# Graph attention layer on one core: all four parts of a strip as bf16 high halves on TensorE and low halves by DMA

## What is computed

```python
q = x @ Wq.T + bq; k = x @ Wk.T + bk; v = x @ Wv.T + bv
scores = q @ k.T / sqrt(128)
scores = where(adj > 0, scores, -9e15)
attention = softmax(scores, axis=-1)
return elu(attention @ v)

h = maximum(layernorm(x), 0)
x = x + L0(h, adj)
h = maximum(layernorm(x), 0)
x = x + L1(h, adj)
```

## Time and profile before

| | |
|---|---|
| median of 3 runs | 781.47 us (781.42 to 786.33) |
| profiled execution | 782.49 us, its span 780.7 us |
| busy in the span | TensorE 93%, VectorE 72%, ScalarE 72%, GpSimd 53% |
| mean granted TensorE clock | 0.977 |
| chain that ended last | third stage, matmuls of line 1337: 30% of the span |

### The profile page before, as it was taken

One profiled execution on the slowest core, in us unless ns is written; L12 is line 12 of the kernel. 1 busy time (PEld: TensorE's weight loads), 2 busy tenths in 40 slices (PEclk: granted clock), 3 DMA queues, 4 the chain that ended last, 5 costly groups with the idle time before them and its releaser, 6 DMA issues. The chain is left out here.

```text
span 780.7 us, 18250 instructions
## 1 busy us (share of the span) xinstructions
PE 728.9 (93%) x6229; PEld 609.6 (78%) x6229; DVE 563.2 (72%) x1199; ACT 559.9 (72%) x1095; POOL 417.6 (53%) x317
## 2 busy tenths in 40 slices
PE   4976999999999999999999998585999999999996
PEld 2555888888888888888888887463888888888885
DVE  4857687878787878878787876498585585586572
ACT  5936678687878777777868787584967977977910
POOL 1058599999999999999999973243000000000000
PEclk9988999999999999999999999797999999999999
DMA  6059989999888898989898954650234334423100
GB/s 229 1 162 280 283 212 248 274 232 280 233 280 238 271 253 254 262 247 256 255 259 245 274 112 73 123 103 1 54 69 93 81 73 91 91 64 87 37 10 13
DMA packets 189323, 130.86 MB, mean 168 GB/s; under 512 B 170336, under 2 KB 176992, under 8 KB 181088
## 3 DMA queue, kind: packets, MB, share of 16 engines
q1 hardware_dynamic: 188544, 130.05, 61.4%
q10 hardware_dynamic: 576, 0.26, 0.1%
q0 software_dynamic: 160, 0.00, 0.0%
HBM read 69.47 MB, written 18.87 MB: 113 GB/s over the span
## 5 line engine op out<-in xcount | busy, mean ns | idle before, releaser
L1337 PE MATMUL ps_x<-v,big 128*128 128x258 bf16 x2048 | 232.0, 275 | 2.3 <-issue 2.3
L1337 PEld LDWEIGHTS ps_x<-v,big 128*128 128x128 fp8e4 x2048 | 198.9, 98 | 32.5 <-issue 2.4
L682 DVE CUSTOM_DVE_ANT_0 scores<-ps_s,mask_neg 128x1024 f32<-128x1024 f32 x128 | 155.7, 1217 | 25.5 <-POOL mask_neg L553 17.0
L538 POOL TENSOR_SCALAR mask_bytes<-adj_sb 128x2048 uint8<-128x2048 int32 x64 | 147.5, 2321 | 44.8 <-POOLq L79 40.9
L601 ACT ACTIVATE scores<-scores,neg_max 128x1024 f32<-128x1024 f32 x128 | 146.1, 1143 | 23.3 <-DVE neg_max L688 23.3
L701 DVE TENSOR_TENSOR low<-scores 128x1024 bf16<-128x1024 f32 x96 | 136.0, 1417 | 29.2 <-ACT scores L601 27.0
L553 POOL TENSOR_SCALAR mask_neg<-mask_bytes 128x2048 bf16<-128x2048 uint8 x64 | 150.6, 2354 | 5.4 <-POOL mask_bytes L538 0.4
L812 PE MATMUL ps_acc<-v_parts,hiT 128*128 128x256 bf16 x768 | 141.6, 274 | 5.4 <-DMA lowT<-low 5.1
L615 ACT ACTIVATE hiT<-ps_t 128x512 bf16<-128x512 bf16 (+1 forms) x128 | 103.0, 805 | 56.6 <-PE ps_t L793 54.0
L878 ACT ACTIVATE big<-s_block,s_col 128x512 fp8e4<-128x512 f32 x224 | 139.3, 714 | 0.0
L813 PE MATMUL ps_acc<-v_parts,lowT 128*128 128x128 bf16 x768 | 134.7, 220 | 0.0
(11 more groups left out here) (139 smaller groups left out, 997.3 us busy)
## 6 DMA issues: line engine op xcount, KB each, us to landing
adj_sb<-in_adj SPq DMA_DIRECT2D x64, 1024.0 KB, 5.3
mask_bytes_dram<-mask_bytes SPq DMA_DIRECT2D x32, 512.0 KB, 2.8
x_sb<-in_x SPq DMA_DIRECT2D x8, 256.0 KB, 7.7
out<-res SPq DMA_DIRECT2D x32, 64.0 KB, 1.5
lowT<-low SPq DMA_TRANSPOSE x96, 4.7
big<-mask_bytes_dram SPq DMA_TRANSPOSE x32, 4.5
raw_w<-in_L_gnn_Wq ACTq DMA_DIRECT2D x1, 64.0 KB, 3.1
raw_w<-in_L_gnn_Wk ACTq DMA_DIRECT2D x1, 64.0 KB, 3.6
```

What stands on the lines that cost most here:

```text
L538: nc.gpsimd.tensor_scalar(mask_bytes[b % 2][:, half(h)], adj_sb[h][:], 1.0, 0.0, ALU.min, ALU.max).then_inc(bytes_ready, 1)
L682: nc.vector.tensor_tensor_reduce(out=scores[bn % 2][:, part(k)], in0=ps_s[k % 2][:], in1=mask[bn % 2][:, part(k)], scale=1.0, scalar=LOWES ...
L1337: last = nc.tensor.matmul(ps_x[b % 2][k][:], by_key_tile(m, t)[:, b], v1[k][:, t, :].bitcast(BF16), start=(t == 0), stop=(t == T - 1))
```

## The change

All four parts of a strip now go the way that parts 0 to 2 went: the bf16 high half is turned on TensorE (UNITS lists the six groups), the low half is made by `low_part` on VectorE and turned by DMA into `lowT`. `turn`, `copy_pT`, `turned_low` and their buffers are gone. `acc_copy` and `add_halves` are replaced by `attended` on VectorE: two operations that scale the two halves of `ps_acc` by the inverse sum out of PSUM and add v's bias. ELU's minus one is subtracted from x once, on GpSimd, while the stage starts, and the subtraction in `add_elu` goes.

```diff
+            UNITS = ((3, slice(0, 512)), (3, slice(512, PART)), (0, slice(0, PART)), (1, slice(0, PART)),
+                     (2, slice(0, 512)), (2, slice(512, PART)))
...
                     def turn_low(c, b, k):
 
                         s = 4 * c + b
-                        sp.wait_ge(low_done, 3 * s + k + 1)
+                        sp.wait_ge(low_done, 4 * s + 1 + (1, 2, 3, 0)[k])
...
-                            sp.wait_ge(pv_done, 8 * s + 2 * k - 4)
+                            sp.wait_ge(pv_done, 8 * s + (-4, -2, 0, -6)[k])
...
                         if has(c, b, 1):
+                            turn_low(*at(c, b, 1), 3)
                             turn_low(*at(c, b, 1), 0)
...
-                    def add_halves(s):
-
-                        pool.wait_ge(acc_out, s + 1)
...
-                        nc.gpsimd.tensor_tensor(acc_sb[:, 0, :], acc_sb[:, 0, :], acc_sb[:, 1, :], ALU.add).then_inc(halves_added, 1)
-                        pool.wait_ge(halves_added, s + 1)
-                        nc.gpsimd.tensor_tensor(att[:], acc_sb[:, 0, :], bv_rep[:], ALU.add).then_inc(att_ready, 1)
-
                     def add_elu(s):
 
-                        steps = Steps(pool, pool_own, 2 * s)
+                        steps = Steps(pool, pool_own, s)
                         pool.wait_ge(att_exp_ready, s + 1)
-                        steps.do(nc.gpsimd.tensor_tensor(att_exp[:], att_exp[:], ones[:], ALU.subtract))
                         steps.do(nc.gpsimd.tensor_tensor(att_exp[:], att_exp[:], att_pos[:], ALU.add))
...
                         make_bytes(0, b)
                         if b < 2:
                             make_mask(0, b)
+                        if b == 1:
+                            flat = x_sb[:].rearrange("p t f -> p (t f)")
+                            nc.gpsimd.tensor_scalar(flat, flat, 1.0, None, ALU.subtract)
...
-                        copy_pT(s, 0)
+                        copy_hiT(s, 0)
                         if has(c, b, 2):
                             copy_q(s + 2, b % 2)
-                        copy_pT(s, 1)
-                        if before:
-                            acc_copy(s - 1, b + 1)
-                        copy_hiT(s, 0)
                         copy_hiT(s, 1)
+                        copy_hiT(s, 2)
+                        copy_hiT(s, 3)
                         if ahead:
                             exps(s + 1, bn, 0)
-                        copy_hiT(s, 2)
+                        copy_hiT(s, 4)
...
-                        copy_hiT(s, 3)
+                        copy_hiT(s, 5)
...
+                    def attended(s):
+
+                        dve.wait_ge(pv_done, 8 * s + 8)
+                        nc.vector.scalar_tensor_tensor(out=acc_sb[:], in0=ps_a[:, 1, :], scalar=inv_by_parity[:, 0:1],
+                                                       in1=bv_rep[:], op0=ALU.mult, op1=ALU.add).then_inc(acc_half, 1)
+                        wait(dve, att_exp_ready, s)
+                        dve.wait_ge(acc_half, s + 1)
+                        nc.vector.scalar_tensor_tensor(out=att[:], in0=ps_a[:, 0, :], scalar=inv_by_parity[:, 0:1],
+                                                       in1=acc_sb[:], op0=ALU.mult, op1=ALU.add).then_inc(att_ready, 1)
...
-                        turned_low(s, 0)
                         low_part(s, b, 1)
                         if ahead:
                             add_mask(s + 1, bn, 2)
-                        turned_low(s, 1)
+                        if has(c, b, -1):
+                            attended(s - 1)
                         low_part(s, b, 2)
...
                         if ahead:
-                            low_part(s + 1, bn, 0)
+                            low_part(s + 1, bn, 3)
                         if ahead2:
                             add_mask(s + 2, (b + 2) % 4, 1)
+                        if ahead:
+                            low_part(s + 1, bn, 0)
...
                     def times_v(s, i):
                         j = PV_ORDER[i]
-                        if i < 2:
-                            pe.wait_ge(pT_low_ready, 2 * s + i + 1)
-                        else:
-                            pe.wait_ge(hiT_ready, 4 * s + (1, 1, 2, 2, 3, 4)[i - 2])
-                            if i % 2 == 0:
-                                pe.wait_ge(lowT_in[j // 2], 16 * s + 16)
+                        pe.wait_ge(hiT_ready, TURNS * s + (1, 2, 3, 3, 4, 4, 5, 6)[i])
+                        if i % 2 == 0:
+                            pe.wait_ge(lowT_in[j // 2], 16 * s + 16)
                         if i == 0:
-                            wait(pe, acc_out, s)
+                            wait(pe, att_ready, s)
...
-                        turn(s, b, 0)
+                        turn_high(s, b, 0)
...
-                        turn(s, b, 1)
+                        turn_high(s, b, 1)
...
-                        turn_high(s, b, 0)
+                        turn_high(s, b, 2)
                         times_v(s, 0)
-                        turn_high(s, b, 1)
+                        turn_high(s, b, 3)
                         times_v(s, 1)
```

More of the change, by code:

```diff
@@ L436, in build @@
                 scores = [sb(c2, f"scores{i}", [D, N], F32) for i in range(2)]
[L437 to L441, removed]
+                hiT = [sb(c2, f"hiT{k}", [D, PART], BF16) for k in range(4)]
+                low = [sb(c2, f"low{k}", [D, PART], BF16) for k in range(4)]
+                lowT = [sb(c2, f"lowT{k}", [D, 8, D], BF16) for k in range(4)]
                 q_strip = [sb(c2, f"q_strip{i}", [D, 2, D], F32R) for i in range(2)]
-                acc_sb = sb(c2, "acc_sb", [D, 2, D], F32)
+                acc_sb = sb(c2, "acc_sb", [D, D], F32)
                 att = sb(c2, "att", [D, D], F32)
@@ L583, in period @@
                             make_mask(*at(c, b, 2))
-                        if has(c, b, -1):
-                            add_halves(4 * c + b - 1)
                         if has(c, b, 3):
@@ L703, in inverse_sum @@
                     def inverse_sum(s, b):
-                        steps = Steps(dve, own, s)
-                        steps.do(nc.vector.tensor_reduce(out=inv_sum[:, b % 2:b % 2 + 1], in_=row_sum[:, b, :], axis=AX.X, op=ALU.add))
-                        wait(dve, acc_out, s - 1)
-                        nc.vector.reciprocal(inv_by_parity[:, b % 2:b % 2 + 1], inv_sum[:, b % 2:b % 2 + 1]).then_inc(inv_ready, 1)
+                        steps = Steps(dve, own, 2 * s)
+                        steps.do(nc.vector.tensor_reduce(out=inv_sum[:, 0:1], in_=row_sum[:, b, :], axis=AX.X, op=ALU.add))
+                        steps.do(nc.vector.reciprocal(inv_by_parity[:, 0:1], inv_sum[:, 0:1]))
+                    def attended(s):
[6 more added lines that the diff above has]
+                                                       in1=acc_sb[:], op0=ALU.mult, op1=ALU.add).then_inc(att_ready, 1)
                     def moments_of(s):
@@ L722, in _ @@
                     add_mask(1, 1, 0)
+                    low_part(0, 0, 3)
                     low_part(0, 0, 0)
@@ L769, in make_scores @@
                         last.then_inc(s_ready, 1)
-                    def turn(s, b, i):
-                        pe.wait_ge(exp_done, 4 * s + 1)
-                        wait(pe, hiT_ready, 4 * (s - 1) + 2 + i)
-                        for t in range(4):
-                            col = 512 * (6 + i) + D * t
-                            last = nc.tensor.transpose(ps_t[i % 3][:, D * t:D * t + D], scores[b % 2][:, col:col + D], ident[:])
-                        last.then_inc(t_done, 1)
                     def turn_high(s, b, u):
-                        k, tiles = ((0, range(8)), (1, range(8)), (2, range(4)), (2, range(4, 8)))[u]
+                        k, half_of = UNITS[u]
                         pe.wait_ge(exp_done, 4 * s + EXP_ORDER.index(k) + 1)
-                        if u == 0:
-                            wait(pe, hiT_ready, 4 * s)
-                        elif u < 3:
-                            pe.wait_ge(pT_low_ready, 2 * s + u)
-                        else:
-                            pe.wait_ge(hiT_ready, 4 * s + 1)
-                        out = ps_t[(2 + u) % 3][:].bitcast(BF16)
+                        wait(pe, hiT_ready, TURNS * s + u - 2)
+                        out = ps_t[u % 3][:].bitcast(BF16)
                         high = high_half(scores[b % 2][:, part(k)])
-                        for t in tiles:
-                            last = nc.tensor.transpose(out[:, D * t:D * t + D], high[:, D * t:D * t + D], ident_half[:])
+                        for col in range(half_of.start, half_of.stop, D):
+                            last = nc.tensor.transpose(out[:, col:col + D], high[:, col:col + D], ident_half[:])
                         last.then_inc(t_done, 1)
```

43 lines of the change are left out of this document (12 added, 31 removed).

## The result

The changed kernel takes 818.35 us (median of 4 runs, 816.33 to 822.0), the kernel before beside it 783.9 us. The ratio is 1.044, with a 95% interval from 1.038 to 1.050: slower. Forecast were 794.0 us and a range of 776 to 809, so the direction was right and the size was not: 34 us more instead of 12.6.

A forecast was written before the change was run, and what follows sets the result against it. TensorE bounded the kernel at 13.32 us per strip; the change would make a two-strip chain bind at 13.76. 26 strips x 0.44 = 11.4, + 3.5 start - 1.3 - 1.0 end = 12.6 us more: 794 us, range 776 to 809.

The forecast's parts named there:

- second chain: Value products, epilogue, mask bytes, load and transpose, closing over two strips: 1.14 us slack before, then 13.76 us per strip.
- TensorE's saving: Two groups of four f32 turns per strip become bf16 turns: 0.43 us less, 13.32 to 12.89 if TensorE bounds.
- attended: Two 128x128 VectorE operations reading PSUM: 0.6 us taken, between nothing and 1.4, with TensorE's wait for them hidden.
- fourth collision: Rival: the fourth low_part also blocks GpSimd near the epilogue, 0.9 us on the chain, 14.21 us per strip, 809; chance 0.16.
- link two: From GpSimd's epilogue start to the mask load's issue on SyncE: 10.48 us before, 8.98 after the change.
- A fourth transpose: On the DMA engines: 0.9 us more per strip, 11.6 to 12.5 us of work, not binding but leaving no room.
- Link one: From a strip's first value products through last turn, copy and exponentials to GpSimd's epilogue start: 9.06 us.
- Link three: From a mask load's issue through the second load to the first transpose's landing: 9.41 us, plus 0.07 to the matmul.
- The two collisions that I left in on link two: GpSimd operations and VectorE's low_part exclude each other, some 0.9 us each time, twice per strip; both kept in.
- Start, 3.5 of 0 to 6.5: Stage start: GpSimd's pass over x, taken as 3.8 us, and the earlier deadline delay strip 0; 3.5 us taken.
- End, -2.3: Last strips: TensorE's saving holds in strips 29 to 31, 1.3 us, and the last epilogue is 1.0 us shorter.

The follow-up runs named there:

- run 8: Run 7's kernel with part 3's eight low-half products on TensorE moved behind part 0's two product groups, nothing left out: 778.19 us, 0.993 of the kernel before.
- run 2: Changed kernel without part 0's DMA transpose, its products reading part 3's turned low half, so three transposes per strip: 812.96 us, 1.036 of the kernel before.
- run 5: Kernel before with a fourth DMA transpose per strip, of a tile nobody reads, issued between those of parts 1 and 2: 792.73 us, 1.013.
- run 6: Changed kernel without the pass over x, right load held until part 3's next low half is made: 803.49 us, 1.022 of the kernel before.
- run 1: Changed kernel without the GpSimd pass that takes one from all of x, ELU's minus one left out: 807.93 us, 1.030 of the kernel before.
- run 3: Changed kernel whose first products read part 3's low half of the strip before, from a second buffer, without waiting: 808.63 us, 1.031 of the kernel before.
- run 7: Changed kernel with part 3's transpose between the two loads and the minus one taken strip by strip on GpSimd: 789.78 us, 1.005 of the kernel before.

## Why the prediction was wrong, point by point

- *What bounds the kernel.* Right. The second chain under TensorE's pace is what the change ran into; every run that shortened it shortened the strip, and with all of its slack back (run 8) TensorE bounds the stage at the predicted pace.
- *TensorE's saving* of 0.43 us a strip: right in size, as far as run 8 shows it: 12.85 us in the strip shown, 13.0 on average, against 13.32. Run 8 moved products too, so the saving isn't measured by itself.
- *attended* as two operations of 0.6 us: 0.343 and 0.350, 0.69 together; no wait worth a line, as said. *low_part* rose from 1427 ns to 1464 on average in the same stretch; its fourth collision, the rival, was not what lengthened the chain, since link two measured 9.00 on average against 8.98.
- *A fourth transpose costs 0.9 us of the DMA engines, which doesn't bind.* It doesn't bind, and in the steady part its price is nothing that can be seen (runs 2, 5 and 8). That it "leaves no room" did not follow: the DMA share, which I read as engines in use, adds up packet times and goes past 1 (1.04 in run 8, in shorter strips).
- *Link one* (9.06) and *link two* (8.98): right within 0.1 (9.07 and 9.00 on average).
- *Link three* (9.41, from a load's issue through the second load to the landing): this is the step that failed. It was taken from before, where the right load comes 2.82 us behind the left one. That distance was itself made by a collision: there both halves of make_bytes took 4.72 us together. The second half, from 319.65 us, met a low_part that had started just ahead of it; after the change the second half starts at 318.63, and it is low_part, behind it, that takes longer. (The two rows stand below this list.) So the pair takes 3.75 us, the right load follows after 1.85, and the landing comes 0.9 us later on average, not 1 us earlier: 10.34 us from the issue to the products where they wait, for 9.48. The two collisions that I left in on link two are still there (1.46 us for the addition, 2.75 for the second half of the mask). This third one lies behind the left load's issue, on no link of mine, and I did not see that it spaced the loads. Nor did I see that the store would come nearer to them, by the averages under run 6 some 0.2 of the 0.9 us. Run 6 puts the distance back and gets link three back where the store is far. Link two then grew to 9.38 in the round shown (314.61 less GpSimd's start at 305.23), so the strip stays at 13.9.
- *Start, 3.5 of 0 to 6.5*: this step failed as well. It is 11.15, of which 8.0 belong to the pass over x. Its price of 3.8 us went by a row of another operation, int32 words to bytes, as if a GpSimd operation on f32 cost the same per element. It took 11.41 us, and it held up VectorE besides, which the sum left out although it named the exclusion for low_part: two low_parts, some 1.4 us each elsewhere, took 11.63 together. The Trainium skill has the exclusion as a rule ("SBUF — State Buffer", section "Who interferes with whom"): a VectorE operation with two inputs in SBUF contends with a GpSimd operation that reads SBUF, and the port pair that they share is an exclusive lock. The trace agrees: of the 11.63 us the second low_part alone took 9.84, beside the pass. (It ended at 72.54 us, 0.65 ahead of the pass's recorded end; ends on GpSimd are rough in this profile.) What the other 3.15 us of the start are was not tried.
- *End, -2.3*: it gave 0.6.

VectorE's low_part beside the second half of make_bytes, before and after:

```profile
319.36 1.40 DVE L701 TENSOR_TENSOR low<-scores 128x1024 bf16<-128x1024 f32 x1 [0.88 <-ACT scores L601]
...
319.52 2.08 DVE L671 TENSOR_TENSOR low<-scores 128x1024 bf16<-128x1024 f32 x1
```

That the measured links add up to two strips is so by construction and proves nothing; what tells is which of them moved. The strips cost 11.9 us more than forecast (23.3 for 11.4), the start 7.65, the end 1.7; strips or start alone would have left the time under 809. The range failed because it gave link three no bounds of its own (it varied collisions on link two, and held the DMA link at one value read in one spacing), and because the start's 6.5 rested on the low price of the pass.

## What to carry to other kernels

A DMA time read from a trace belongs to what stood ahead of it in the queue and at what distance; when a change moves the issues, that time needs bounds like any unknown. A new transfer that is needed early goes ahead of large loads, or its consumers go later: here those two edits, with the minus one taken strip by strip, turned 1.030 (run 1) into 0.993 (run 8). And an operation on a slow engine over a whole tensor is priced by a row of the same type and engine, or bounded widely, with what it locks out.

## What the runs showed of the hardware

- A DMA transpose issued behind two loads of 1 MB landed 0.95 to 1.06 us after the second load, in every pair after 200 us of the two kernels and of runs 1, 2, 3, 5 and 6, whatever the distance of the loads.
- With the store of 0.5 MB 1.9 to 2.3 us ahead, loads 1.85 us apart had that landing 10.16 us after the first issue (run 2), loads 2.83 and 3.1 apart 9.27 and 9.45 (runs 5 and 6). With the store 0.7 and 1.1 us ahead, loads 3.0 and 3.1 us apart had 11.3 and 10.6 (run 6).
- In the gap ahead of a late landing few packets start (20 to 68 GB/s for 0.5 to 1.5 us, at two places of the changed kernel), while packets of the transposes stand for up to 2.1 us until the load's last are through. What delays those was not settled.
- A GpSimd tensor_scalar over 128x4096 f32 took 11.41 us (2.8 ns per element of a partition) beside two low_parts, so its price by itself is not shown; 128x2048 int32 to bytes take 1.89 (0.9 ns).
- A 128x128 subtraction on GpSimd took 0.47 us in the epilogue, and 0.45 to 1.54 us, 1.01 on average, behind the bytes (run 7), where low_part can run beside it. That the two exclude each other there is an inference from the start, not shown by a run of its own.
